# A 1-core transformer kernel: the first group of token attention in two halves, and weight loads issued behind the next rows' load

## The chip, the core and the metric

The kernel runs on one core of a Trainium2 chip. A core has a matmul engine (TensorE, PE in the profile), a vector engine (DVE), a scalar engine (ACT), GpSimd (POOL) and a sync engine (SP), which here issues all DMAs. Each engine works through its own instructions in order, and semaphores tie them together. The metric is the device time of one execution in microseconds (us).

## The reference

Three layers one after the other: attention over time steps inside each of 64 batches (the part that the change touches), a windowed attention over features, and a gated network with ternary weights.

```python
def _L0_tok_ref(qkv):                      # qkv is x: 64 x 96 x 512
    ch = qkv.shape[1] // 3                 # 32
    q, k, v = jnp.split(qkv, 3, axis=1)
    scale = 1.0 / np.sqrt(np.sqrt(ch)).astype(np.float32)
    weight = jnp.einsum('bct,bcs->bts', q * scale, k * scale)
    weight = jax.nn.softmax(weight.astype(jnp.float32), axis=-1).astype(weight.dtype)
    return jnp.einsum('bts,bcs->bct', weight, v)
...
h = _L0_tok_ref(x)
h = h + _L0_attn_ref(_layernorm(h, axis=-1), Wq, Wk, Wv, Wo, qn_w, kn_w)
h = h + _L0_ffn_ref(_layernorm(h, axis=-1), w1, w2, w3)
```

The second layer needs a scale for each attention weight matrix (from the largest absolute value), the third the mean absolute value of each of its matrices. The kernel measures both on the chip while the first layer runs.

## The kernel before

**Groups.** Token attention takes the 64 batches in 16 groups of 4 (`NG`, `GB`). A group has 16 (`STEPS`) row blocks and 16 column blocks of scores, each 128 x 512.

**Splitting and stacking.** The scores are made from fp32 numbers split in a high and a low part. `load_qk(g)` (L268) brings the raw q and k of a group (512 KB). ACT writes the high part (`raise_`, L418), POOL the low part (`lower`, L370), and `stack(g)` (L276 to L282) is six SBUF-to-SBUF copies of 256 KB that set high and low parts on interleaved partitions of `q_parts` and `k_parts`, 96 partitions in all. The raw rows of all groups but group 1 go through one buffer, `qk_split`, so `load_qk(g)` waits until `stack(g-1)` has landed.

**Rows, maxima, columns.** `rows(g, k)` (L625) makes one row block of scores; DVE reduces it to 128 row maxima (`maximum`, L473). After the 16 row blocks PE turns the maxima over (`transpose_maxima`, L631), DVE negates and splits them (`max_hi`, L480, and `max_lo`, L482), and SP stores them as partitions 96 and 97 of `q_parts` (`store_max`, L296, two DMAs of 8 KB). `cols(g, u)` (L640) makes the transposed scores with the maxima already subtracted; its first one in a group waits for both stores. ACT takes the exponentials (`exps`, L434), and `weigh(g, i)` (L650) multiplies four of them with v at the steps of `OUT_AT`. `total` (L659, L662) sums for the denominators.

**The order on PE.** The code is a hand-written pipeline. In group g, step u runs from 2 to 17. A step makes one row block of a later group (rows of group g+1 up to its last, then from step 11 on rows of group g+2), one column block (from step 16 on those of group g+1), and what `OUT_AT` adds. The transpose of the maxima of group g+1 stands in step 12. `score_ring` numbers the uses of the three PSUM banks of row scores in this order.

**The order on SP.** One queue, in program order. Round g of its loop: `stack(g+2)`, the v rows, the weight chunks that are measured in group g+1 (2 attention chunks of 512 KB where g+1 is even, 3 where it is odd, and 1 feed-forward chunk of 704 KB, up to group 7), `load_qk(g+3)`, the store of a finished group (`store_h`, 256 KB), and `store_max(g+1)`. The chunks of group 0 (2 and 1) are issued ahead of the loop. Their DMAs are L301 and L306.

**The order on ACT.** The exponentials step by step; after step 13 `raise_(g+3)`; the chunks' measurements (`bound_attn`, L438, and `sum_ffn`, L443) at the steps 3, 8, 12 and 5.

## Time and profile before

| | us |
|---|---|
| median of 3 runs | 1065.02 |
| lowest and highest of them | 1060.88, 1065.99 |
| the profiled execution's own time | 1062.14 |
| its span in the profile | 1060.3 |

| engine | busy us | share of the span |
|---|---|---|
| PE, matmul | 972.8 | 92% |
| DVE | 728.4 | 69% |
| POOL | 489.7 | 46% |
| ACT | 449.9 | 42% |

Token attention lies in the first 340 us or so; the two later layers fill the rest. A timeline row gives the start, the duration, the engine and source line, the tiles written and read, and in brackets how long the engine had been idle before and what ended that.

### The profile page before, as it was taken

What the parts mean: (1) busy time and instruction counts of PE and PEld (TensorE: products, weight loads), DVE (VectorE), ACT (ScalarE), POOL (GpSimd) and SP (SyncE); (2) the same over time, 40 slices, a digit from 0 to 9 for tenths busy, and PEclk for the clock granted to TensorE, in tenths of its full rate; (3) what the DMA queues carried; (4) which work ended last, traced back from release to release, by engine and by line L of the source; (5) the groups of instructions that cost most, each with busy time, mean ns of one, the idle gap of its engine ahead of it and who ended that gap; (6) DMA issues with size and microseconds to landing.
All of it is one profiled execution on the core that took longest, in us unless ns stands there. A gap on an engine that the chain in (4) does not pass through costs nothing.

```text
span 1060.3 us, 20456 instructions
## 1 busy us (share of the span) xinstructions
PE 972.8 (92%) x7799; PEld 523.1 (49%) x7799; DVE 728.4 (69%) x1265; ACT 449.9 (42%) x761; POOL 489.7 (46%) x373
## 2 busy tenths in 40 slices
PE   4998989887887589999999999999999999999986
PEld 1433333332332236566466564664655646646555
DVE  5675767887888877676675776766756767567542
ACT  1676766676775444333242233332432333323221
POOL 2243434355757764544346345443463454434500
PEclk9998999999998889999999999999999999999998
DMA  8996976667533313223223132231231322312300
GB/s 219 269 298 198 294 241 187 198 182 207 155 134 112 89 27 65 64 59 74 50 59 73 46 69 62 57 79 45 54 79 49 69 59 58 81 45 46 72 20 21
DMA packets 157483, 113.14 MB, mean 107 GB/s; under 512 B 126336, under 2 KB 126976, under 8 KB 157440
## 3 DMA queue, kind: packets, MB, share of 16 engines
q1 hardware_dynamic: 157440, 112.59, 39.5%
q8 instruction: 24, 0.39, 0.2%
q14 instruction: 19, 0.16, 0.0%
HBM read 49.36 MB, written 8.39 MB: 54 GB/s over the span
## 4 chain that ended last, share of the span: by engine, by line
PE 60%; issue 3%; DVE 3%; POOL 2%; DMA 1%; SPq 1%; ACT 1%; POOLq 0%; DVEq 0%; ACTq 0%
PE ffn_sum L1428 7%; PE ffn_sum L1429 7%; PE proj L1491 5%; PE proj L1486 5%; PE proj L1487 5%; PE proj L1375 4%; PE proj L1377 4%; PE proj L1376 4%; PE transposed L1457 3%; PE transposed L1458 3%; PE ffn_sum L1377 3%; PE ffn_sum L1376 3%; PE ffn_sum L1375 3%; PE ffn_sum L1471 2%; PE transposed L1375 1%
## 5 line engine op out<-in xcount | busy, mean ns | idle before, releaser
L1009 POOL TENSOR_TENSOR roped<-rope_cos,rope_sin 128x512 f32<-128x512 f32 x80 | 107.7, 1347 | 246.9 <-DVE rope_sin L1209 246.9
L473 DVE TENSOR_REDUCE row_max<-score_rows 128x1 f32<-128x512 f32 x256 | 163.0, 677 | 47.7 <-PE score_rows L625 47.7
L434 ACT ACTIVATE exps<-score_cols 128x512 f32<-128x512 f32 x256 | 140.2, 600 | 92.3 <-PE score_cols L640 89.4
L1428 PE MATMUL ffn_sum<-x_hi,ffn_w 128*128 128x128 f16 x1408 | 162.4, 221 | 8.0 <-DMA x_lo<-x_lo_rows 8.0
L1429 PE MATMUL ffn_sum<-x_lo,ffn_w 128*128 128x128 f16 x1408 | 162.2, 221 | 0.0
L625 PE MATMUL score_rows<-k_parts,q_parts 96*128 96x512 f32 x256 | 121.7, 491 | 29.4 <-DMA k_parts<-qk_split 14.1
L1428 PEld LDWEIGHTS ffn_sum<-x_hi,ffn_w 128*128 128x128 f16 x1408 | 138.0, 98 | 11.8 <-DMA x_lo<-x_lo_rows 8.4
L1429 PEld LDWEIGHTS ffn_sum<-x_lo,ffn_w 128*128 128x128 f16 x1408 | 138.6, 98 | 1.8
L640 PE MATMUL score_cols<-q_parts,k_parts 98*128 98x512 f32 x256 | 107.9, 429 | 12.7 <-DMA q_parts<-max_lo 7.8
L379 POOL TENSOR_TENSOR exp_sums<-exps 128x512 f32<-128x512 f32 x64 | 84.0, 1343 | 65.4 <-PE score_rows L625 39.3
L625 PEld LDWEIGHTS score_rows<-k_parts,q_parts 96*128 96x128 f32 x256 | 52.1, 205 | 120.4 <-DVE row_max L473 68.7
L1486 PE MATMUL proj<-attn_slots,ctx_hi 128*128 128x512 f16 x256 | 98.2, 383 | 4.8 <-ACT ctx_hi L1126 3.2
L1487 PE MATMUL proj<-attn_slots,ctx_hi 128*128 128x512 f16 x256 | 98.2, 384 | 0.0
L1021 POOL TENSOR_TENSOR roped_lo_rows<-roped,roped_hi_rows 128x512 f16<-128x512 f32 x77 | 90.5, 1192 | 0.0
L1092 ACT ACTIVATE squares<-ffn_sum 128x512 f32<-128x512 f32 x32 | 19.1, 598 | 159.9 <-PE ffn_sum L1377 159.9
L1363 DVE SCALAR_TENSOR_TENSOR h<-proj,o_unscale,h_res 128x512 f32<-128x512 f32 x16 | 12.0, 751 | 99.3 <-PE proj L1491 99.3
L1240 DVE SCALAR_TENSOR_TENSOR x2n_tanh_hidden<-x2n_tanh_hidden,ffn_sum 128x512 f32<-128x512 f32 (+1 forms) x48 | 30.8, 641 | 68.1 <-PE ffn_sum L1429 68.1
L1375 PE MATMUL proj<-attn_slots,x_hi 128*128 128x512 f16 x192 | 73.9, 385 | 3.3 <-DMA x_lo<-x_lo_rows 3.3
L650 PE MATMUL tok_out<-exps,v_t 128*32 128x512 f32 x512 | 72.2, 637 | 4.5 <-ACT exps L434 4.4
L1377 PE MATMUL proj<-attn_slots,x_lo 128*128 128x512 f16 x192 | 73.9, 385 | 0.0
L1376 PE MATMUL proj<-attn_slots,x_hi 128*128 128x512 f16 x192 | 73.9, 385 | 0.0
L90 POOL TENSOR_TENSOR attn_slots<-attn_slots 128x1024 f16<-128x1024 f32 x20 | 47.6, 2378 | 54.5 <-ACT attn_slots L86 54.5
(154 smaller groups left out, 1897.1 us busy)
## 6 DMA issues: line engine op xcount, KB each, us to landing
q_parts<-qk_split SPq DMA_DIRECT2D x45, 256.0 KB, 4.2
k_parts<-qk_split SPq DMA_DIRECT2D x45, 256.0 KB, 4.7
attn_slots<-in_w_attn SPq DMA_DIRECT2D x20, 512.0 KB, 7.0
ffn_w<-in_w_ffn SPq DMA_DIRECT2D x13, 704.0 KB, 8.3
qk_split<-in_qk SPq DMA_DIRECT2D x15, 512.0 KB, 5.9
raw_ffn<-in_w_ffn SPq DMA_DIRECT2D x8, 704.0 KB, 6.9
v_t<-in_v_t SPq DMA_DIRECT2D x16, 256.0 KB, 5.6
h_rows<-tok_out_sum SPq DMA_DIRECT2D x16, 256.0 KB, 3.4
```

The costliest lines, as they stand in the source:

```text
L434: nc.scalar.activation(E[:, n % NE, :], ST[n % 3][:, :], ACT.Exp, scale=TOK_SCALE).then_inc(exp_done, 1)
L473: nc.vector.reduce_max(row_max[:, g % 2, k:k + 1], S[n % NS][:, :], AX.X).then_inc(s_free, 1)
L625: nc.tensor.matmul(bank[:, :], QP[g % NB][0:3 * CH, b, t * P:(t + 1) * P], KP[g % NB][0:3 * CH, b, :], start=True, stop=True).then_inc(s_f ...
L640: nc.tensor.matmul(ST[n % 3][:, :], KP[g % NB][0:3 * CH + 2, b, i * P:(i + 1) * P], QP[g % NB][0:3 * CH + 2, b, :], start=True, stop=True) ...
L1009: nc.gpsimd.tensor_tensor(rope[:, c, :], ra[c % 2][:, :], rb[c % 2][:, :], ALU.add).then_inc(added, 1)
L1375: nc.tensor.matmul(dst, ah, bh, start=(i == 0), stop=False)
L1376: nc.tensor.matmul(dst, ah, bl, start=False, stop=False)
L1377: t = nc.tensor.matmul(dst, al, bh, start=False, stop=(i == len(pairs) - 1))
L1428: nc.tensor.matmul(dst, w, x2h[:, k, :], start=(k == 0), stop=False)
L1429: ins = nc.tensor.matmul(dst, w, x2l[:, k, :], start=False, stop=(k == KD - 1))
L1486: nc.tensor.matmul(PROJ[1][:, :], ch[:, k, :], W.hi(at, D), start=(k == 0), stop=False)
L1487: nc.tensor.matmul(PROJ[1][:, :], ch[:, k, :], W.lo(at, D), start=False, stop=False)
```

## The change

Four things change.

1. **The first group comes in halves.** The host lays out group 0 so that batches 0 and 1 are on the first 64 partitions. ACT raises q and k of group 0 apart, POOL lowers q and DVE lowers k. `stack_first` makes two times six copies of 128 KB, first for batches 0 and 1, then for 2 and 3. The row maxima of group 0 are turned over, split and stored in two halves of 8 row blocks each (`transpose_half`, `take_half`, `store_half_max`). The column blocks of group 0 are taken in the order of `FIRST_COLS`, whose first six need only the first half. PE makes 1 row block of group 1 instead of 7 before the first column block, and two in each of steps 2 to 6 (`rows_beside`).
2. **The queue of SP.** `stack(1)` is issued directly behind the copies of group 0. `load_qk(2)` moves behind the first half's maxima and the v rows of group 0, and `raise_(2)` behind the first two exponentials. In each round of the loop `load_qk(g+3)` stands in front of the weight chunks. The chunks of group 0 are no longer issued ahead of the loop but in round 0, together with those of group 1.
3. **The measurements.** ACT measures attention chunks at steps 4, 7 and 10 and the feed-forward chunk at step 15 (in group 0: 10 and 14, and 16).
4. **Waits.** Semaphore counts are moved by the one more raise and the one more pair of stores.

```diff
+HALF = STEPS // 2
+HALF_TAKE = HALF + 1
+FIRST_COLS = [(0, 0), (0, 1), (1, 0), (1, 1), (2, 0), (2, 1), (0, 2), (0, 3), (1, 2), (1, 3), (2, 2), (2, 3),
+              (3, 0), (3, 1), (3, 2), (3, 3)]
+SECOND_HALF = 6
+
+
+def col_of(g, u):
+
+    return FIRST_COLS[u] if g == 0 else divmod(u, GB)
+
+
+def exps_needed(g, pairs):
+
+    return STEPS * g + 1 + max(u for u in range(STEPS) if col_of(g, u) in pairs)
+
+
+def rows_beside(g, u):
+
+    if g == 0 and u < LOOK:
+        return [(1, 2 * u - 2), (1, 2 * u - 1)]
+    if u < MAX_AT:
+        return [(g + 1, u - 2 + LOOK)] if g + 1 < NG else []
+    return [(g + 2, u - MAX_AT)] if g + 2 < NG else []
+
...
 def score_ring():
 
-    entries = [("row", 0, k) for k in range(STEPS)]
-    for k in range(LOOK):
-        entries += [("row", 1, k)] + ([("max", 0)] if k == TAKE else [])
+    entries = []
+    for k in range(STEPS):
+        entries += [("row", 0, k)] + ([("half_max", 0)] if k == HALF_TAKE else [])
+    entries += [("row", 1, 0), ("row", 1, 1), ("max", 0)]
     for g in range(NG):
         for u in range(2, STEPS + 2):
-            if u < MAX_AT and g + 1 < NG:
-                entries.append(("row", g + 1, u - 2 + LOOK))
-            if u >= MAX_AT and g + 2 < NG:
-                entries.append(("row", g + 2, u - MAX_AT))
+            entries += [("row", *at) for at in rows_beside(g, u)]
             if u == MAX_AT + TAKE and g + 1 < NG:
                 entries.append(("max", g + 1))
...
-        A_MEASURE_AT, F_MEASURE_AT, CONVERT_AT = (3, 8, 12), (5,), (3, 12, 16, 8)
+        A_MEASURE_AT, F_MEASURE_AT, CONVERT_AT = (4, 7, 10), (15,), (3, 12, 16, 8)
+        FIRST_A_MEASURE_AT, FIRST_F_MEASURE_AT = (10, 14), (16,)
...
-        OUT_AT = {8: 0, 10: 1, 13: 2, 17: 3}
+        OUT_AT, FIRST_OUT_AT = {8: 0, 10: 1, 13: 2, 17: 3}, {9: 0, 11: 1, 13: 2, 17: 3}
...
                 if g == 2:
+                    sp.wait_ge(half_stacked, COPIES)
                     sp.wait_ge(stacked[0], copies(0))
...
+            def stack_first(half):
+                done, bs = (half_stacked, stacked[0])[half], slice(2 * half, 2 * half + 2)
+                of = slice(half * 2 * CH, half * 2 * CH + 2 * CH)
+                high, low = split_high(0).bitcast(FP32), split_low(0).bitcast(FP32)
+                sp.wait_ge(hi_done, 1)
+                sp.dma_start(QP[0][0:3 * CH:3, bs, :].bitcast(FP32), high[of, 0, :]).then_inc(done, DMA)
+                sp.dma_start(QP[0][1:3 * CH:3, bs, :].bitcast(FP32), high[of, 0, :]).then_inc(done, DMA)
+                sp.wait_ge(hi_done, 2)
+                sp.dma_start(KP[0][0:3 * CH:3, bs, :].bitcast(FP32), high[of, 1, :]).then_inc(done, DMA)
+                sp.dma_start(KP[0][2:3 * CH:3, bs, :].bitcast(FP32), high[of, 1, :]).then_inc(done, DMA)
+                sp.wait_ge(lo_done, 1)
+                sp.dma_start(QP[0][2:3 * CH:3, bs, :].bitcast(FP32), low[of, 0, :]).then_inc(done, DMA)
+                sp.wait_ge(k_lo_done, 1)
+                sp.dma_start(KP[0][1:3 * CH:3, bs, :].bitcast(FP32), low[of, 1, :]).then_inc(done, DMA)
+
             def load_v(g):
                 if g >= NV:
                     sp.wait_ge(out_done, NT * (g - NV + 1))
                 sp.dma_start(VT[g % NV][:, :, :].rearrange("p i n -> p (i n)"), vt[g, :, :]).then_inc(v_in[g % NV], DMA)
 
+            def store_half_max(half):
+                bs = slice(2 * half, 2 * half + 2)
+                for part, of in enumerate((max_hi, max_lo)):
+                    if part == 0:
+                        sp.wait_ge(max_split, half + 1)
+                    else:
+                        sp.wait_ge(s_free, ring["max" if half else "half_max", 0] + 1)
+                    row = QP[0][3 * CH + part:3 * CH + part + 1, bs, :].bitcast(FP32)
+                    sp.dma_start(row, of[0:HALF, :].bitcast(FP32)).then_inc(max_in, DMA)
+
...
             sp.dma_start(ident[:, :], ident_in).then_inc(ident_in_sem, DMA)
-            stack(0)
+            stack_first(0)
+            stack_first(1)
+            stack(1)
+            store_half_max(0)
+            load_v(0)
             load_qk(2)
-            stack(1)
-            load_v(0)
+            store_half_max(1)
             load_v(1)
-            for c in A_MEASURED[0]:
-                load_attn(c)
-            for c in F_MEASURED[0]:
-                measure_ffn(c)
-            store_max(0)
             for g in range(NG):
                 if g + 2 < NG:
                     stack(g + 2)
                 if 0 < g and g + 1 < NG:
                     load_v(g + 1)
+                if g + 3 < NG:
+                    load_qk(g + 3)
+                for c in A_MEASURED[0] if g == 0 else ():
+                    load_attn(c)
+                for c in F_MEASURED[0] if g == 0 else ():
+                    measure_ffn(c)
                 for c in A_MEASURED[g + 1] if g + 1 < NG else ():
                     load_attn(c)
                 for c in F_MEASURED[g + 1] if g + 1 < NG else ():
@@ -350,8 +406,6 @@
                     sp.wait_ge(h_out, DMA)
                     rows1.load(sp, 0, h1[0:P, :])
                     rows1.load_constants(sp, tables_in, norm_in, mask_in)
-                if g + 3 < NG:
-                    load_qk(g + 3)
                 if g > 0:
                     store_h(g - 1)
                 if g + 1 < NG:
...
         @block.scalar
         def _(act):
+            def raise_first(m):
+                act.wait_ge(qk_in[0], DMA)
+                nc.scalar.copy(split_high(0)[:, m, :], split_raw(0)[:, m, :]).then_inc(hi_done, 1)
+
             def raise_(g):
                 act.wait_ge(qk_in[g % 2], DMA * (g // 2 + 1))
                 if g == 2:
+                    act.wait_ge(half_stacked, COPIES)
                     act.wait_ge(stacked[0], copies(0))
...
                         act.wait_ge(s_full, ring["den", was] + 1)
-                if n == NE - 4:
+                i, b = col_of(g, u)
+                if g == 0 and (i, b) == (2, 0):
                     act.wait_ge(stacked[1], copies(1))
-                nc.scalar.activation(E[:, n % NE, :], ST[n % 3][:, :], ACT.Exp, scale=TOK_SCALE).then_inc(exp_done, 1)
+                nc.scalar.activation(E[:, (STEPS * g + GB * i + b) % NE, :], ST[n % 3][:, :], ACT.Exp, scale=TOK_SCALE).then_inc(exp_done, 1)
...
             def bound_attn(c):
                 act.wait_ge(a_in[c % NA], DMA * (c // NA + 1))
+                if c > 0:
+                    act.wait_ge(a_stat, c)
...
 
-            for g in range(3):
-                raise_(g)
+            raise_first(0)
+            raise_first(1)
+            raise_(1)
             exps(0, 0)
             exps(0, 1)
+            raise_(2)
             for g in range(NG):
                 for u in range(2, STEPS + 2):
                     if u < STEPS:
@@ -455,8 +525,8 @@
                         exps(g + 1, u - STEPS)
                     if u == SPLIT_AT and g + 3 < NG:
                         raise_(g + 3)
-                    for at, chunks, what in ((A_MEASURE_AT, A_MEASURED[g], bound_attn),
-                                             (F_MEASURE_AT, F_MEASURED[g], sum_ffn),
+                    for at, chunks, what in ((A_MEASURE_AT if g else FIRST_A_MEASURE_AT, A_MEASURED[g], bound_attn),
+                                             (F_MEASURE_AT if g else FIRST_F_MEASURE_AT, F_MEASURED[g], sum_ffn),
...
-            nc.vector.memset(ones[:, :], 1.0).then_inc(const_set, 1)
             for n in range(NB):
+                if n == 1:
+                    dve.wait_ge(hi_done, 2)
+                    nc.vector.tensor_tensor(split_low(0)[:, 1, :], split_raw(0)[:, 1, :], split_high(0)[:, 1, :].bitcast(FP32),
+                                            ALU.subtract).then_inc(k_lo_done, 1)
+                    nc.vector.memset(ones[:, :], 1.0).then_inc(const_set, 1)
...
-                    if k == TAKE and r >= 1:
+                    if (r, k) == (0, HALF_TAKE):
+                        take_half(0)
+                    if (r, k) == (1, TAKE):
+                        take_half(1)
+                    if k == TAKE and r >= 2:
...
-                if k == 0:
+                if (g, k) == (0, 0):
+                    pe.wait_ge(half_stacked, COPIES)
+                elif k == 0 or (g, k) == (0, HALF):
                     pe.wait_ge(stacked[g % 2], copies(g))
                 bank = enter_ring(ring["row", g, k])
...
 
+            def transpose_half(half):
+                last = half * HALF + HALF
+                pe.wait_ge(s_free, ring["row", 0, last - 1] + 1)
+                bank = enter_ring(ring["max" if half else "half_max", 0])
+                nc.tensor.transpose(bank[0:HALF, 0:P], row_max[:, 0, last - HALF:last], ident[:, :]).then_inc(s_full, 1)
...
-                    pe.wait_ge(max_in, 2 * DMA * (g + 1))
+                i, b = col_of(g, u)
+                if (g, u) == (0, 0):
+                    pe.wait_ge(const_set, 1 + NB)
+                    pe.wait_ge(max_in, 2 * DMA)
+                elif u == 0 or (g, u) == (0, SECOND_HALF):
+                    pe.wait_ge(max_in, 2 * DMA * (g + 2))
                 if n >= 3:
...
+                out_at = FIRST_OUT_AT if g == 0 else OUT_AT
+                if u in out_at:
+                    weigh(g, out_at[u])
...
 
-            pe.wait_ge(ident_in_sem, DMA)
-            pe.wait_ge(const_set, 1 + NB)
             for k in range(STEPS):
                 rows(0, k)
-            for k in range(LOOK):
-                rows(1, k)
-                if k == TAKE:
-                    transpose_maxima(0)
+                if k == HALF_TAKE:
+                    pe.wait_ge(ident_in_sem, DMA)
+                    transpose_half(0)
+            rows(1, 0)
             cols(0, 0)
+            rows(1, 1)
+            transpose_half(1)
...
```

**SP's queue from the last stacking copy of group 2 to the maxima of group 1, before.** L282 is that copy, L301 and L306 are weight chunks, L268 the raw rows of group 3, L296 the maxima:

```order
L282 DMA k_parts<-qk_split 32x4x512
L301 DMA attn_slots<-in_w_attn 128x1024 x3
L306 DMA ffn_w<-in_w_ffn 128x1408
L268 DMA qk_split<-in_qk 128x1024 [waits t_stacked0]
L296 DMA q_parts<-max_hi 1x16x128 [waits t_max_split]
L296 DMA q_parts<-max_lo 1x16x128 [waits t_s_free]
```

The same piece now (L309 the last copy, L295 the raw rows, L353 and L358 the chunks, L348 the maxima):

```order
L309 DMA k_parts<-qk_split 32x4x512
L295 DMA qk_split<-in_qk 128x1024 [waits t_stacked0]
L353 DMA attn_slots<-in_w_attn 128x1024 x2
L358 DMA ffn_w<-in_w_ffn 128x1408
L353 DMA attn_slots<-in_w_attn 128x1024 x3
L358 DMA ffn_w<-in_w_ffn 128x1408
L348 DMA q_parts<-max_hi 1x16x128 [waits t_max_split]
L348 DMA q_parts<-max_lo 1x16x128 [waits t_s_free]
```

The raw rows have moved ahead of the chunks, and three chunks (two attention, one feed-forward) have come in that stood ahead of this piece before.

**SP's queue ahead of that piece, now:** from the last copy of group 1 (L309) over the maxima of the two halves (L339), the v rows (L329) and the raw rows of group 2 (L295) to the first copy of group 2 (L303):

```order
L309 DMA k_parts<-exps 32x4x512
L339 DMA q_parts<-max_hi 1x8x128 [waits t_max_split]
L339 DMA q_parts<-max_lo 1x8x128 [waits t_s_free]
L329 DMA v_t<-in_v_t 128x512
L295 DMA qk_split<-in_qk 128x1024 [waits t_stacked0,t_half_stacked]
L339 DMA q_parts<-max_hi 1x8x128 [waits t_max_split]
L339 DMA q_parts<-max_lo 1x8x128 [waits t_s_free]
L329 DMA v_t<-in_v_t 128x512
L303 DMA q_parts<-qk_split 32x4x512 [waits t_hi_done]
```

Before, the v rows, two attention chunks and a feed-forward chunk stood between the copies of group 1 and one pair of maxima, and the raw rows of group 2 were issued ahead of the copies of group 1.

**ACT in group 0, before** (L434 exponentials, L438 attention chunk, L443 feed-forward chunk):

```order
L434 ACTIVATE exps<-score_cols 128x512 [waits t_st_done] x4
L438 ACTIVATE attn_slots,w_bound<-attn_slots 128x1024 [waits w_a_in0]
L434 ACTIVATE exps<-score_cols 128x512 [waits t_st_done] x2
L443 ACTIVATE ffn_w,w_fsum<-ffn_w 128x1408 [waits w_fm_in0]
L434 ACTIVATE exps<-score_cols 128x512 [waits t_st_done] x2
```

and now (L483 is the raise, L500 the exponentials, L506 the attention chunk):

```order
L500 ACTIVATE exps<-score_cols 128x512 [waits t_st_done] x2
L483 CAST qk_split<-qk_split 128x1024 [waits t_stacked0,t_half_stacked,t_qk_in0]
L500 ACTIVATE exps<-score_cols 128x512 [waits t_st_done] x2
L500 ACTIVATE exps<-score_cols 128x512 [waits t_stacked1,t_st_done]
L500 ACTIVATE exps<-score_cols 128x512 [waits t_st_done] x6
L506 ACTIVATE attn_slots,w_bound<-attn_slots 128x1024 [waits w_a_in0]
L500 ACTIVATE exps<-score_cols 128x512 [waits t_st_done]
```

The raise of group 2 has come in behind the second exponential, and the first chunk is measured behind the eleventh instead of the fourth.

## Rows read from the trace of the kernel before

**Rows 1.** Stretch, length, busy PE, PEld, DVE, ACT, POOL; granted clock, DMA share, GB/s.
```profile
400.00:1060.00 660.00, 645.21 (x6121) 388.06 (x6119) 426.26 (x783) 204.98 (x360) 289.09 (x245) 0.99 0.26 58
```

**Rows 2.** Timeline, all engines, from the start to the first column block.
```profile
5.03 0.71 SPq L276 DMA_DIRECT2D q_parts<-qk_split  x1
...
8.38 0.61 SPq L282 DMA_DIRECT2D k_parts<-qk_split  x1
...
14.12 9.52 PE L625 MATMUL score_rows<-k_parts,q_parts 96*128 96x512 f32 x16 [14.12 <-DMA k_parts<-qk_split]
...
20.98 0.43 SPq L306 DMA_DIRECT2D ffn_w<-in_w_ffn  x1
...
25.06 1.22 PE L625 MATMUL score_rows<-k_parts,q_parts 96*128 96x512 f32 x2 [1.43 <-DMA k_parts<-exps]
...
27.10 0.27 DVE L480 TENSOR_SCALAR max_hi<-score_rows 16x128 fp32r<-16x128 f32 x1
...
31.62 1.22 PE L640 MATMUL score_cols<-q_parts,k_parts 98*128 98x512 f32 x2 [1.89 <-DMA q_parts<-max_lo]
```

**Rows 3.** Timeline, PE, group 0: columns 6, third weighing, first columns of group 1.
```profile
36.48 0.63 PE L640 MATMUL score_cols<-q_parts,k_parts 98*128 98x512 f32 x1
...
43.16 1.06 PE L650 MATMUL tok_out<-exps,v_t 128*32 128x512 f32 x8
...
45.79 0.50 PE L640 MATMUL score_cols<-q_parts,k_parts 98*128 98x512 f32 x1 [0.20 <-DMA q_parts<-max_lo]
```

**Rows 4.** Timeline, SP: issues of round 0, then of round 2.
```profile
28.67 0.61 SPq L276 DMA_DIRECT2D q_parts<-qk_split  x1
...
37.86 0.33 SPq L268 DMA_DIRECT2D qk_split<-in_qk  x1
...
63.01 0.61 SPq L276 DMA_DIRECT2D q_parts<-qk_split  x1
...
71.92 0.33 SPq L268 DMA_DIRECT2D qk_split<-in_qk  x1
...
78.24 0.59 SPq L296 DMA_DIRECT2D q_parts<-max_lo  x1
```

**Rows 5.** DMA issues of 18 to 31.6 us: count, KB each, median us to landing.
```profile
ffn_w<-in_w_ffn SPq DMA_DIRECT2D x1, 704.0 KB, 10.1
q_parts<-max_hi SPq DMA_DIRECT2D x1, 8.0 KB, 3.2
q_parts<-max_lo SPq DMA_DIRECT2D x1, 8.0 KB, 3.5
```

**Rows 6.** The same for single issues: at 78.24, 134.84 and 164.40 us.
```profile
q_parts<-max_lo SPq DMA_DIRECT2D x1, 8.0 KB, 3.6
...
q_parts<-max_lo SPq DMA_DIRECT2D x1, 8.0 KB, 1.9
...
qk_split<-in_qk SPq DMA_DIRECT2D x1, 512.0 KB, 3.2
```

**Rows 7.** Busy time by stretch, columns as in rows 1.
```profile
36.90:43.60 6.70, 6.70 (x36) 2.94 (x38) 4.89 (x10) 6.60 (x13) 4.89 (x4) 1.00 1.02 402
79.40:81.80 2.40, 0.57 (x3) 0.13 (x1) 1.54 (x3) 0.97 (x2) 0.00 (x0) 0.96 0.07 22
81.80:88.00 6.20, 6.16 (x19) 2.40 (x23) 2.08 (x3) 3.33 (x8) 2.37 (x1) 0.50 0.82 191
```

**Rows 8.** Timeline, PE: the first columns of groups 2, 3, 4 and 7.
```profile
62.93 0.50 PE L640 MATMUL score_cols<-q_parts,k_parts 98*128 98x512 f32 x1 [0.18 <-DMA q_parts<-max_lo]
...
81.84 0.80 PE L640 MATMUL score_cols<-q_parts,k_parts 98*128 98x512 f32 x1 [1.87 <-DMA q_parts<-max_lo]
...
102.62 0.50 PE L640 MATMUL score_cols<-q_parts,k_parts 98*128 98x512 f32 x1 [0.95 <-DMA q_parts<-max_lo]
...
155.48 0.50 PE L640 MATMUL score_cols<-q_parts,k_parts 98*128 98x512 f32 x1 [1.84 <-DMA q_parts<-max_lo]
```

**Rows 9.** Timeline, ACT: the raise of group 5.
```profile
80.83 1.04 ACT L418 CAST qk_split<-qk_split 128x1024 fp32r<-128x1024 f32 x1 [2.60 <-DMA qk_split<-in_qk]
```

51 lines of the change are left out of this document (31 added, 20 removed).

## The prediction

> **What bounds the kernel now.** I read the busy times first. From 400 us to the end PE is busy 645 of 660 us [rows 1], and nothing there is tied to a clock time, so whatever moves the end of token attention moves the end of the kernel by as much. So the question is when each group's first column block starts. I call that moment C0 for group 0, C1 for group 1, and so on.
>
> Next the timeline of the start. The first stacking copy is issued at 5.03, the sixth at 8.38, and the row blocks start at 14.12: 9.1 us after the first issue. They run at one per 0.6 us. Group 1's copies hold the next rows until 25.06, the maxima are split at 27.10 and C0 is 31.62 [rows 2]. C1 is 45.79 [rows 3]. C1 to C2 takes 17.14 us, and PE waited only 0.2 us for the maxima there [rows 3, 8]: the undisturbed pace of a group. C3 and C7 come late, each after an idle PE of 1.9 us behind the maxima's store [rows 8].
>
> Then the DMA engines. The copies are slow, the loads fast: from 36.90 to 43.60 the loads of round 0 move 402 GB/s at a DMA share of 1.02 [rows 7]. They are full, and the maxima's store goes into the same queue. An 8 KB store lands in 1.9 us when the queue is empty, in 3.5 to 3.6 us when weight chunks are ahead of it [rows 5, 6].
>
> **The start (half stacking).** A half is six copies of 128 KB. SP issues one per 0.67 us (3.35 us for five steps [rows 2]), so the first half is issued from about 4.6 to 8.6 us and lands near 10.7. The rows of batches 0 and 1 hide the second half: eight blocks of 0.6 us against 4 us of issue. Twelve issues end at 12.5, stack(1) is issued by 16.4. All three move 3.15 MB; one stack of 1.57 MB took 9.1 us of which I take 7.3 for its bytes, so stack(1) lands near 21. The first half's maxima are ready at 17.8 but their store is queued behind stack(1), so it lands at about 21.8, and **C0 is 22.0, 9.6 us earlier**. PE is then six row blocks behind the old order. They cost DVE time in steps 2 to 6: five steps with two blocks, ten of 0.65 us, from 24.4. Column block 6 comes at 29.7 against 36.48 [rows 3]. The second half's maxima (split at 24.2, landed near 26.7) are in time. So 6.8 us are left of the gain there. Bounds: stack(1) cannot land before its last issue plus 3.2 us, 19.5 (C0 at 20.3); if 128 KB copies have a fixed cost of their own, C0 is 24.
>
> **Round 0 (the weights moved).** This is where I expect the gain to go. raise_(2) now stands behind the second exponential, which is done at 24.9, so stack(2) is issued from 26.2 (C0 + 4.2). A stack's landing frees load_qk 8.9 to 9.2 us after its first issue [rows 4]: 35.2 us. Only behind load_qk(3) do the chunks come, and they are five attention and two feed-forward chunks instead of three and one. First bytes come about 0.9 us after the issue (an estimate: 1.9 us for 8 KB, part of it before the first byte). From 36.1: 0.52 + 5 x 0.52 + 2 x 0.72 = 4.6 MB at 402 GB/s is 11.4 us, so the engines are full until 47.5. store_max(1) stands behind all of them on SP and in the queue. It would be issued at 39, in time for a C1 of 39.0 (29.7 + the 9.3 us from 36.48 to 45.79 [rows 3]). It lands 2 us behind the end of the backlog: in round 2 the loads ended at 79.4 and PE went on at 81.84 (2.4 us) [rows 7, 8], and at the start the store of max_lo landed 3.5 us after its issue [rows 5]. So **C1 is 49.5, 3.7 us later than before** instead of 6.8 earlier. Bounds: t(stack 2) from C0 at 20.3 gives 47.8, C0 at 24 gives 51.5; a price of zero for the backlog is the first rival below.
>
> ACT waits too: attention chunk 0 is measured at step 10, at 33.5 us, but lands at 35.2 + 3.2 + 1.3 = 39.7. With 1.3 us for the measurement the eleventh exponential ends at 41.6, and the third weighing waits for it, some 3 us. That lies inside the wait for C1 and costs nothing as long as the store lands later than 44.2.
>
> The order of landing in the queue rests on two stores, so I weighed it against a page. The feed-forward chunk issued at 20.98 landed 10.1 us later, at 31.1; max_hi, issued after the split at 27.4, landed 3.2 us later at 30.6, so ahead of the chunk, max_lo at 31.5, behind it [rows 2, 5]. The Trainium skill (DMA: Bandwidth & Descriptors, "Queues, rings and completion order") says that each DMA engine takes its descriptors in ring order, but that completion is not first in, first out over a queue. The trace agrees, with half a microsecond. By that rule C1 would be up to 1 us earlier, 48.5.
>
> **After C1.** PE stands idle for about 5.5 us (from 44 to 49.5). After the 1.87 us before C3, the granted clock was 0.50 for the next 6.2 us [rows 7], the lower of its two levels, 1.2 GHz; C3 to C4 took 20.78 us, 3.64 over the pace, of which 0.77 is the longer wait at C4 [rows 8]. So the clock cost 2.9. I put 2.9 behind C1. Bounds: 0 and 2.9.
>
> **Rounds 1 to 6.** Taking load_qk out of the tail removes the wait of ACT at 80.83 [rows 9]. But in before that wait ran beside the wait for the maxima, which ended later, at 81.84 [rows 8]. It is not worth anything alone. What sets C3 is the end of the backlog: stack issued 63.01, loads ended 79.4, 16.4 later [rows 4, 7]. Now the chunks wait for the stack to land. Between the v rows' last bytes and load_qk's first the engines stand still, 1.0 us (bounds 0.6 and 1.9, the whole latency of a small store). The same bytes then end 17.4 us after the stack's issue and the store lands 2.2 later, at 19.6. The stack is issued 0.8 us before C2, since no measurement stands at step 12 any more, so the store lands 18.8 us after it against a pace of 17.1: **a wait of 1.7 us in each round with three attention chunks** (2, 4, 6). With two chunks 1.3 us less is to be moved, and nothing waits. Before, waits of 1.87 and 1.84 us lowered the clock, one of 0.95 didn't [rows 8]; I count two thirds of 2.9 us for each of the two that fall between C2 and C7. That is 3 x 1.7 + 2 x 1.9 = 9.0 us over the pace between C2 and C7, where before had 92.55 - 5 x 17.14 = 6.85 [rows 8]. So **2.1 us more**. The measurements' new steps, the self-wait of bound_attn and the halved raises lie beside PE work and cost nothing; ACT has 42% of the span.
>
> **Sum.** 3.7 + 2.9 + 2.1 = 8.7 us. Against the execution's own 1062.1 that is 1070.8 us; the median of the runs is 2.9 us above that execution. I say 1071; this case's own range is 1066 to 1077.
>
> **The rivals.**
> 1. The store passes the weights (it waits for little more than its own 1.9 us). Then ACT's late measurement sets C1 at 41.6 + 2.6 = 44.2, 1.6 earlier than before, no clock is lost and rounds 2 to 6 run at the pace: -1.6 - 6.85 = -8.5, **1053.6**. It decides if the store of group 1's maxima lands within 5 us of its issue. For it: a max_hi landed ahead of an older chunk. Against it: both stores with chunks ahead took 3.5 us, not 1.9. Chance 0.14 (with other ways of a gain).
> 2. C1 is late as forecast, but the later rounds keep the pace, because ring order hurts less with load_qk gone from the tail: 3.7 + 2.9 - 6.85 = -0.3, **1062**. Chance 0.25.
> 3. C1 late and the waits of 1.7 us come, but the clock stays up after them: 6.6 + 5.1 - 6.85 = +4.9, **1067**. Chance 0.15.
> 4. The waits also come with two chunks (0.7 us each) and every one lowers the clock, or C0 is 24: +14, **1076**. Chance 0.10.
> 5. The forecast, 1071: 0.36.
>
> **How the numbers follow.** About 0.5% (5.3 us) is what a measurement of this kernel can tell from no change. Faster by more: rival 1 and the low tail of rival 2, 0.17. Within: the rest of rival 2, most of rival 3 and the low edge of the forecast, 0.35. Slower: 0.48. The range leaves out rival 1 and the far end of rival 4: 1056 to 1078.
>
> **What would show it.** C0 near 22; the first half's rows from 10.7; the raw rows of group 3 issued near 35; PE idle before C1 "<-DMA q_parts<-max_lo" for over 4 us, with the DMA share at 1.0 until 47 and the granted clock at 0.50 after it; C1 near 49.5; waits of 1 to 2 us before C3, C5 and C7. A C1 before 46 breaks the forecast, and so does a store of group 1's maxima that lands within 5 us.

## The result and the profile after

| | before | after |
|---|---|---|
| median of the runs, us | 1064.99 | 1083.7 |
| lowest and highest, us | 1060.88, 1065.99 | 1079.23, 1088.35 |
| runs | 4 | 4 |

The ratio is 1.0199, with a 95% interval of 1.014 to 1.0257: the changed kernel is slower by 2%. The prediction was 1071 with a range up to 1078. The sign was right and the size too small by more than half. The profiled execution took 1088.35 us, with a span of 1086.5. Some executions of a kernel are over 1.5% longer than its fastest; the ratios here and below leave these out, and two of the four of f1_before_order, its traced one (1088.22 us) among them, are such.

The later layers are as they were. The same length of time near the end, now shifted by 20 us, against [rows 1] (columns as there):

```profile
420.00:1080.00 660.00, 648.74 (x6138) 390.03 (x6137) 428.92 (x790) 206.17 (x362) 290.72 (x248) 0.99 0.26 59
```

So the loss is in token attention. PE at the start, against [rows 2, 3]: the first row blocks, the first column block, and column block 6, counted from 0 as the 36.48 of [rows 3] is.

```profile
10.88 5.96 PE L715 MATMUL score_rows<-k_parts,q_parts 96*128 96x512 f32 x10 [10.88 <-DMA k_parts<-qk_split]
...
23.17 0.70 PE L739 MATMUL score_cols<-q_parts,k_parts 98*128 98x512 f32 x1
...
30.40 0.39 PE L739 MATMUL score_cols<-q_parts,k_parts 98*128 98x512 f32 x1
```

Rows start at 10.88, C0 is 23.17 instead of 31.62, and column block 6 comes 6.1 us earlier than before. The halves do what they are meant to do. Then SP in round 0 and round 2, against [rows 4]:

```profile
27.09 0.62 SPq L303 DMA_DIRECT2D q_parts<-qk_split  x1
...
36.11 0.33 SPq L295 DMA_DIRECT2D qk_split<-in_qk  x1
36.49 0.91 SPq L353 DMA_DIRECT2D attn_slots<-in_w_attn  x2
...
70.35 0.60 SPq L303 DMA_DIRECT2D q_parts<-qk_split  x1
...
79.26 0.33 SPq L295 DMA_DIRECT2D qk_split<-in_qk  x1
79.63 1.38 SPq L353 DMA_DIRECT2D attn_slots<-in_w_attn  x3
...
81.55 0.45 SPq L373 DMA_DIRECT2D h_rows<-tok_out_sum  x1
...
85.92 0.66 SPq L348 DMA_DIRECT2D q_parts<-max_lo  x1
87.43 0.62 SPq L303 DMA_DIRECT2D q_parts<-qk_split  x1
```

The raw rows are issued 9.0 and 8.9 us after the first stacking copy, and the chunks directly behind them. PE and ACT next, against [rows 3, 8]: ACT at the first chunk, and PE at the third weighing and the first column blocks of groups 1, 3, 5 and 7.

```profile
41.13 1.06 ACT L506 ACTIVATE attn_slots<-attn_slots 128x1024 f32<-128x1024 f32 x1 [6.22 <-DMA attn_slots<-in_w_attn]
...
42.81 1.69 PE L749 MATMUL tok_out<-exps,v_t 128*32 128x512 f32 x8 [2.16 <-ACT exps L500]
...
51.24 0.80 PE L739 MATMUL score_cols<-q_parts,k_parts 98*128 98x512 f32 x1 [4.44 <-DMA q_parts<-max_lo]
...
94.11 0.80 PE L739 MATMUL score_cols<-q_parts,k_parts 98*128 98x512 f32 x1 [6.49 <-DMA q_parts<-max_lo]
...
133.03 0.79 PE L739 MATMUL score_cols<-q_parts,k_parts 98*128 98x512 f32 x1 [3.33 <-DMA q_parts<-max_lo]
...
173.67 0.80 PE L739 MATMUL score_cols<-q_parts,k_parts 98*128 98x512 f32 x1 [4.20 <-DMA q_parts<-max_lo]
```

C1 is 5.5 us late. The waits before C3, C5 and C7 are 6.49, 3.33 and 4.20 us, where before had 1.87 and 1.84 at C3 and C7 and 0.95 at C4. Busy time of the six groups from C2 to C8 (length; then PE, PEld, DVE, ACT, POOL; granted clock, DMA share, GB/s):

```profile
70.75:94.11 23.36, 16.14 (x89) 6.70 (x89) 13.32 (x24) 14.50 (x26) 8.88 (x6) 0.93 0.95 264
94.11:112.81 18.70, 17.74 (x90) 7.14 (x90) 11.76 (x21) 12.59 (x23) 5.96 (x5) 0.90 0.52 172
112.81:133.03 20.22, 16.14 (x89) 6.69 (x89) 13.31 (x24) 14.46 (x26) 8.86 (x6) 0.97 0.93 267
133.03:152.58 19.55, 18.59 (x90) 7.58 (x90) 11.84 (x21) 12.70 (x23) 5.96 (x5) 0.86 0.72 203
152.58:173.67 21.09, 16.14 (x90) 6.69 (x90) 13.31 (x24) 14.47 (x26) 8.88 (x6) 0.98 0.93 270
173.67:193.38 19.71, 18.76 (x90) 7.58 (x90) 11.85 (x21) 12.70 (x23) 5.96 (x5) 0.85 0.35 97
```

A group that begins behind a long wait shows a mean clock of 0.85 to 0.90 and takes 18.7 to 19.7 us instead of 17.1; a group with three chunks ends in the wait and takes 20.2 to 23.4. In the groups with three chunks the DMA engines are busy 93 to 95% of the time. C2 to C8 is 122.6 us against 111.3 before. C8 is 193.38 against 174.26, 19.1 us late, and the medians differ by 18.7: about all of the loss is there by C8. The two traced executions are 26.2 us apart, since from C8 to the last weighing the changed kernel took 168.2 us and before 160.3. But that stretch takes 154 to 169 us in the seventeen traces used here, with no order that follows the edits. From here on C8 and the stretch from C2 to C8 are what I compare.

Round 2 in pieces (columns as above):

```profile
79.00:80.00 1.00, 0.52 (x2) 0.30 (x2) 1.00 (x3) 1.00 (x3) 0.76 (x2) 1.00 0.24 86
80.00:81.00 1.00, 1.00 (x9) 0.16 (x8) 1.00 (x3) 1.00 (x2) 1.00 (x2) 1.00 0.75 176
81.00:86.00 5.00, 5.00 (x31) 2.06 (x27) 4.18 (x9) 3.87 (x9) 2.25 (x2) 1.00 1.05 369
86.00:88.00 2.00, 1.62 (x9) 0.87 (x5) 1.45 (x4) 1.87 (x4) 1.08 (x1) 1.00 0.94 351
88.00:90.00 2.00, 0.00 (x0) 0.00 (x0) 0.62 (x2) 1.41 (x3) 1.27 (x1) 1.00 1.00 329
90.00:94.00 4.00, 0.00 (x0) 0.00 (x0) 0.00 (x0) 0.00 (x0) 0.00 (x0) 0.61 1.06 228
```

From 79 to 80 the DMA engines nearly stand still. Then they load at 369 and 351 GB/s. PE stops at 88, and by 90 the rate has fallen to 228 GB/s: that is the six copies of the next stack, issued from 87.43 on, in front of which the maxima's store still has not landed. The granted clock goes to its lower level while PE stands.

The last two transfers in front of the store are the feed-forward chunk, issued at 81.07, and the h rows, issued at 81.55 (columns as in [rows 6]):

```profile
ffn_w<-in_w_ffn SPq DMA_DIRECT2D x1, 704.0 KB, 11.9
h_rows<-tok_out_sum SPq DMA_DIRECT2D x1, 256.0 KB, 12.1
```

They land at 93.0 and 93.7, and PE goes on at 94.11. In all rounds that I read this way (round 2 of before, after, e1, e4, f1, g1 and g4, rounds 4 and 6 of after and e4) PE went on 0.3 to 0.6 us after the h rows had landed. So the store lands with the last of the transfers in front of it, which can be some 2 us after most engines are through.

### The profile page after: what moved, and what is told of

The parts are those of the page before. It is cut to its first block, busy times and chain, and to the rows that moved or that the text cites. A ratio compares the mean times of both kernels' runs of the same rounds, so it can differ in the third digit from the quotient of the medians.

```text
span 1086.5 us, 20494 instructions
## 1 busy us (share of the span) xinstructions
PE 986.5 (91%) x7800; PEld 527.1 (49%) x7800; DVE 728.3 (67%) x1268; ACT 452.2 (42%) x762; POOL 487.5 (45%) x373
## 4 chain that ended last, share of the span: by engine, by line
PE 58%; issue 3%; DVE 3%; POOL 2%; DMA 1%; SPq 1%; ACT 1%; POOLq 0%; DVEq 0%; ACTq 0%
PE ffn_sum L1526 7%; PE ffn_sum L1527 7%; PE proj L1589 5%; PE proj L1584 5%; PE proj L1585 4%; PE proj L1473 4%; PE proj L1474 4%; PE proj L1475 4%; PE transposed L1555 3%; PE transposed L1556 3%; PE ffn_sum L1475 3%; PE ffn_sum L1473 3%; PE ffn_sum L1474 3%; PE ffn_sum L1569 2%; PE transposed L1473 1%
## 5 line engine op out<-in xcount | busy, mean ns | idle before, releaser
L500 ACT ACTIVATE exps<-score_cols 128x512 f32<-128x512 f32 x256 | 141.9, 598 | 126.3 <-PE score_cols L739 123.8
L715 PE MATMUL score_rows<-k_parts,q_parts 96*128 96x512 f32 x256 | 124.1, 498 | 27.4 <-DMA k_parts<-qk_split 12.7
L739 PE MATMUL score_cols<-q_parts,k_parts 98*128 98x512 f32 x256 | 111.7, 443 | 28.0 <-DMA q_parts<-max_lo 20.0
L438 POOL TENSOR_TENSOR exp_sums<-exps 128x512 f32<-128x512 f32 x64 | 82.1, 1309 | 89.3 <-PE score_rows L715 75.7
L715 PEld LDWEIGHTS score_rows<-k_parts,q_parts 96*128 96x128 f32 x256 | 53.5, 209 | 123.1 <-DVE row_max L543 64.6
L1190 ACT ACTIVATE squares<-ffn_sum 128x512 f32<-128x512 f32 x32 | 19.1, 598 | 159.6 <-PE ffn_sum L1475 159.6
L749 PE MATMUL tok_out<-exps,v_t 128*32 128x512 f32 x512 | 76.0, 669 | 4.6 <-ACT exps L500 4.5
L739 PEld LDWEIGHTS score_cols<-q_parts,k_parts 98*128 98x128 f32 x256 | 52.6, 207 | 50.3 <-DMA q_parts<-max_lo 28.5
```

The source lines that it names most:

```text
L500: nc.scalar.activation(E[:, (STEPS * g + GB * i + b) % NE, :], ST[n % 3][:, :], ACT.Exp, scale=TOK_SCALE).then_inc(exp_done, 1)
L715: nc.tensor.matmul(bank[:, :], QP[g % NB][0:3 * CH, b, t * P:(t + 1) * P], KP[g % NB][0:3 * CH, b, :], start=True, stop=True).then_inc(s_f ...
L739: nc.tensor.matmul(ST[n % 3][:, :], KP[g % NB][0:3 * CH + 2, b, i * P:(i + 1) * P], QP[g % NB][0:3 * CH + 2, b, :], start=True, stop=True) ...
```

## Experiments

The tables give the start of the first column blocks C1 and C8, the wait before C1 and those before C3, C5 and C7, the length from C2 to C8 (all from the profiled execution), and the time and ratio to the kernel before. Runs of one batch were on one chip; the kernel before had 1057.88 us (first four), 1061.3 (next four), 1060.45 (next four) and 1060.34 (last three). The column "us" is the median of all executions of a kernel: 2 for g1 and h1, 4 for before, after, e2, e4, f1 and f3, 10 or 12 for the others.

| kernel | C1 | wait C1 | waits C3, C5, C7 | C2 to C8 | C8 | us | ratio (interval) |
|---|---|---|---|---|---|---|---|
| before | 45.79 | 0.20 | 1.87, 0.17, 1.84 | 111.3 | 174.3 | 1064.99 | 1 |
| after | 51.24 | 4.44 | 6.49, 3.33, 4.20 | 122.6 | 193.4 | 1083.7 | 1.0199 (1.014 to 1.0257) |
| e1_order_back | 47.31 | 4.63 | 1.54, 0.21, 1.66 | 107.9 | 177.0 | 1061.64 | 1.0027 (0.9989 to 1.0066) |
| e2_chunks_early | 47.54 | 1.79 | 5.51, 3.13, 4.66 | 121.6 | 187.8 | 1075.52 | 1.0163 (1.0097 to 1.023) |
| e3_both | 43.91 | 0.32 | 1.47, 0.18, 1.75 | 108.9 | 173.3 | 1061.8 | 1.003 (0.9993 to 1.0067) |
| e4_copies_wait | 50.77 | 3.68 | 4.16, 3.53, 4.85 | 123.1 | 194.0 | 1081.63 | 1.0213 (1.0133 to 1.0293) |
| f1_before_order | 49.04 | 3.37 | 4.78, 3.74, 4.25 | 122.5 | 191.0 | 1083.0 | 1.0131 (1.0069 to 1.0193) |
| f2_before_actstore | 45.35 | 0.25 | 1.38, 0.95, 1.80 | 106.4 | 168.9 | 1057.13 | 0.9952 (0.9921 to 0.9984) |
| f3_after_actstore | 47.53 | 1.04 | 0.16, 0, 0; see below | 115.8 | 186.2 | 1070.91 | 1.0102 (1.0062 to 1.0142) |
| f4_both_actstore | 44.70 | 0 | 1.23, 0.40, 1.68 | 108.2 | 170.7 | 1057.97 | 0.9984 (0.9951 to 1.0018) |
| g1_half_chunks | 48.77 | 4.94 | 1.62, 0.97, 0.16 | (see below) | | 1072.65 | 1.0106 (1.001 to 1.0203) |
| g2_h_behind | 45.36 | 0.17 | 1.18, 0.51, 1.32 | 112.0 | 174.6 | 1060.88 | 0.9989 (0.9944 to 1.0035) |
| g3_h_behind_act | 45.54 | 0.23 | 1.49, 1.00, 1.56 | 114.5 | 177.1 | 1061.21 | 0.9997 (0.9958 to 1.0037) |
| g4_one_ahead | 48.59 | 7.31 | 2.73, 2.09, 2.70 | 115.1 | 182.3 | 1070.44 | 1.0105 (1.0063 to 1.0146) |
| h1_act_copies_wait | 48.25 | 0.94 | 2.09, 3.41, 3.87 | 120.7 | 191.1 | 1079.0 | 1.0179 (1.0111 to 1.0246) |
| h2_steps_actstore | 45.41 | 0.23 | 1.68, 0.15, 1.72 | 110.9 | 173.9 | 1056.54 | 0.9976 (0.995 to 1.0001) |
| h3_steps_only | 45.95 | 0.17 | 1.69, 0.18, 1.66 | 109.4 | 172.5 | 1057.21 | 0.9977 (0.9946 to 1.0009) |

### Which part of the change: undoing the order, undoing the place of group 0's chunks, both

Two theories after the result: A, the stacking copies of the next group get ahead of the maxima's store; B, the raw rows' place leaves the engines idle for 1 us.

e1_order_back:

```diff
-                if g + 3 < NG:
-                    load_qk(g + 3)
                 for c in A_MEASURED[0] if g == 0 else ():
...
+                if g + 3 < NG:
+                    load_qk(g + 3)
                 if g > 0:
                     store_h(g - 1)
```

> The changed kernel with load_qk(g+3) moved back behind the weight chunks in every round of the loop; all else as changed. Theory A (the next stacking copies are now issued right behind the maxima's store and get ahead of it, because the raise no longer waits for rows at the tail of the queue): the waits before the first columns of groups 3, 5 and 7 (6.5, 3.3 and 4.2 us in the changed kernel) fall to at most 2 us, since the raise is gated by the tail again; the first columns of group 1 stay near 50 us, and the time falls by 8 to 13 us, to about 1072. Theory B (only the idle gap of about 1 us before load_qk in the DMA engines matters): each of the three waits falls by 1 us, the time by 3 to 5 us, to about 1079.

The rounds go back to what they were before, or better: C2 to C8 takes 107.9 us, and the ratio goes from 1.0199 to 1.0027. That is far more than theory B's 3 to 5 us, and more than theory A's 8 to 13 too: C1, which was to stay near 50, is 3.9 us earlier. C1 to C2 takes 21.8 us here, since `load_qk(3)` stands behind seven chunks in round 0.

e2_chunks_early issues group 0's three chunks ahead of the loop, behind `load_qk(2)`:

```diff
             load_qk(2)
+            for c in A_MEASURED[0]:
+                load_attn(c)
+            for c in F_MEASURED[0]:
+                measure_ffn(c)
             store_half_max(1)
```

> The changed kernel with the three weight chunks of group 0 issued ahead of the loop again, behind load_qk(2); all else as changed. Both theories: the backlog in front of group 1's maxima is 1.77 MB smaller, 4.4 us at 402 GB/s, so the first columns of group 1 come at about 47 instead of 51.2 us, and PE's wait there shrinks from 4.4 to below 1 us; the time falls by 4 to 7 us, to about 1078. If the rounds' delay does not depend on when the first ends, the waits of groups 3, 5 and 7 stay at 3 to 6 us. If the chunks of group 0 are not the cause of the late group 1, nothing changes.

C1 comes 3.7 us earlier, behind a wait of 1.79 us where under 1 was expected, and that is all: the waits of the later rounds stand. The two parts are separate, and the second is the small one.

e3_both has both edits, so that of the change the halves, the place of the first stacking copies and the new measurement steps are left.

> Both of the two edits before: load_qk behind the weight chunks and the chunks of group 0 ahead of the loop; what is left of the change is the half-wise start, the stacking order at the start, and the measuring steps. Theory A: the sum of the two gains, 12 to 20 us, so at or below the kernel before: 1060 to 1070, with the first columns of group 1 near 43 us (before 45.8). Theory B: 1072 to 1076.

C1 is 1.9 us earlier than before, all that is left of a C0 that is 8 us earlier, and C2 gives it back: C1 to C2 takes 20.45 us. PE in group 0 and ACT at the raise of group 3:

```profile
36.73 0.73 PE L715 MATMUL score_rows<-k_parts,q_parts 96*128 96x512 f32 x1 [2.47 <-DMA k_parts<-qk_split]
...
43.53 1.05 ACT L483 CAST qk_split<-qk_split 128x1024 fp32r<-128x1024 f32 x1 [1.64 <-DMA qk_split<-in_qk]
```

The copies of group 2 hold PE for 2.47 us at 36.73, and the raise of group 3 waits for its rows at 43.53. The early start meets a supply that has not become earlier.

e4_copies_wait tests theory A: the copies of the next group wait until the maxima have landed.

```diff
+                if 0 < g and g + 2 < NG:
+                    sp.wait_ge(max_in, 2 * DMA * (g + 2))
                 if g + 2 < NG:
                     stack(g + 2)
```

> The changed kernel with one more wait on the issuing queue: stack(g+2) is issued only when both stores of group g's maxima have landed (from round 1 on); the order of the loads stays as changed. Theory A: the copies can no longer get ahead of the store, so the waits before groups 3, 5 and 7 fall from 6.5, 3.3 and 4.2 us to 2 to 2.5 us, the time by 4 to 8 us. Theory B, or a store that is late only because of the chunks in front of it: the waits keep their length, the stacking comes later, and the time stays or grows by up to 5 us.

The wait before C3 falls by 2.3 us, those before C5 and C7 do not, and the time stays. Theory A is not the main cause. With the copies gone from the tail, round 2 can be read cleanly: first copy issued at 70.85, most engines through with the loads at 89.5, C3 at 91.92.

```profile
79.00:81.00 2.00, 1.40 (x10) 0.46 (x10) 2.00 (x4) 2.00 (x5) 1.75 (x3) 1.00 0.51 132
81.00:86.00 5.00, 5.00 (x31) 2.06 (x27) 4.17 (x9) 3.87 (x9) 2.37 (x2) 1.00 0.97 360
86.00:89.00 3.00, 1.76 (x9) 0.87 (x5) 2.21 (x4) 2.87 (x5) 1.95 (x1) 1.00 0.96 330
89.00:90.00 1.00, 0.00 (x0) 0.00 (x0) 0.00 (x0) 0.54 (x2) 0.40 (x1) 1.00 0.53 198
90.00:92.00 2.00, 0.08 (x1) 0.08 (x1) 0.00 (x0) 0.00 (x0) 0.00 (x0) 0.75 0.10 37
```

The h rows, issued at 83.12, land at 91.5 here:

```profile
h_rows<-tok_out_sum SPq DMA_DIRECT2D x1, 256.0 KB, 8.4
```

### The order alone, on the kernel before

f1_before_order:

```diff
+                if g + 3 < NG:
+                    load_qk(g + 3)
                 for c in A_MEASURED[g + 1] if g + 1 < NG else ():
                     load_attn(c)
...
-                if g + 3 < NG:
-                    load_qk(g + 3)
                 if g > 0:
                     store_h(g - 1)
```

> The kernel before with one edit: in each round of SP's loop the raw rows' load (load_qk(g+3)) stands in front of the weight chunks. Theory C (the order alone is the cause: the chunks wait until the stack has landed, so their bytes end right at the maxima's store): C2 to C8 takes 120 to 124 us instead of 111.3, C1 comes up to 2 us later since group 0's three chunks still go ahead of the loop, waits of 3 to 6 us stand before C3, C5 and C7, and the time is 1070 to 1077 where before has 1058 to 1065, so a ratio of 1.009 to 1.014. Theory D (the order costs only together with the new measurement steps and the halves): C2 to C8 takes 113 us or less and the ratio is under 1.004.

C2 to C8 takes 122.5 us, as in the changed kernel. One line of order in the queue makes the whole loss of the rounds; e1 says the same from the other side. f1's traced execution took 1088.22 us where two others took 1070.52 and 1077.78, but 897 us of it lie behind C8, against 888 in before, so much of the extra length is not in the rounds. In time the order alone costs 1.3%, less than the 2.0% of the whole change, with intervals that overlap. Its C1 is 3.3 us later than before, where up to 2 were expected. Round 2 of the undone order (e1, first copy issued at 68.72) and of the order alone (f1, 68.42), first e1, then f1:

```profile
77.00:79.00 2.00, 1.25 (x11) 0.46 (x10) 2.00 (x5) 2.00 (x6) 1.76 (x2) 1.00 1.02 376
79.00:85.00 6.00, 6.00 (x37) 2.49 (x30) 4.69 (x9) 4.12 (x8) 2.59 (x3) 1.00 1.02 408
85.00:87.00 2.00, 0.96 (x5) 0.44 (x3) 1.88 (x3) 0.52 (x1) 0.00 (x0) 1.00 0.12 40
```

```profile
77.00:79.00 2.00, 1.76 (x11) 0.55 (x11) 2.00 (x5) 2.00 (x6) 2.00 (x3) 1.00 0.51 130
79.00:88.00 9.00, 6.46 (x32) 2.83 (x32) 6.01 (x11) 5.76 (x10) 4.09 (x3) 1.00 1.00 355
88.00:90.00 2.00, 0.00 (x0) 0.00 (x0) 0.00 (x0) 0.00 (x0) 0.00 (x0) 0.65 1.06 219
```

In e1 the chunks are already queued when the copies are through, so the engines pass to them without a break, move 376 to 408 GB/s and most are through at 85.1. In f1 they move 130 GB/s for two microseconds, then 355, and are not through when the next copies (issued at 85.25) come in at 88; then it is 219 GB/s.

### How much a byte in front of the store costs

g1_half_chunks:

```diff
-                sp.dma_start(W.raw(c), w_attn[:, c * A_CHUNK:(c + 1) * A_CHUNK])
+                sp.dma_start(W.raw(c)[:, 0:A_CHUNK // 2], w_attn[:, c * A_CHUNK:c * A_CHUNK + A_CHUNK // 2])
...
+                if g == 7:
+                    for c in range(A_CHUNKS):
+                        load_rest(c)
```

> The changed kernel, but each attention chunk's load in the rounds brings half of its columns (256 KB), and only that half is measured; the other halves are all loaded in round 7, so only groups 0 to 7 are to be compared. Measuring the second halves is left out. Theory G (the waits are the length of the backlog that stands between the stack's landing and the maxima): a round with three chunks has 0.79 MB less, 2.1 to 2.3 us at 340 to 385 GB/s, so the waits before C3, C5, C7 fall from 6.5, 3.3, 4.2 to about 4, 1.2, 2.0, the one before C1 (five chunks, 1.3 MB less) from 4.4 to 1, and C2 to C8 is 110 to 116 us instead of 122.6. Theory H (the waits come from the order of issue and landing as such, or from the next stack's copies): they change by less than 0.7 us each, C2 to C8 stays over 119 us.

The three waits fall by 4.9, 2.4 and 4.0 us, 3.8 on the mean, more than the 2.1 to 2.3 us of the bytes; a new wait of 1.24 us before C6 takes some of it back, so that the waits from C3 to C7 fall by 3.4 us a round. C2 to C7 takes 91.6 us (102.9 in the changed kernel, 92.6 before). C8 cannot be used, since the other halves are loaded there. The wait before C1, which was to fall to 1 us, rose from 4.44 to 4.94: C1 itself is 2.5 us earlier, but PE reached it at 43.8 instead of 46.8, since ACT began on the first chunk 1.6 us sooner and measured only half of it, and the copies of group 3 were issued from 43.63 on, again ahead of the landing. A likely reason for the surplus is in the windows: most engines are through with round 2 at 83.9, before the copies issued at 84.08 move a byte.

```profile
78.00:84.00 6.00, 6.00 (x32) 2.68 (x31) 4.62 (x10) 4.17 (x7) 2.04 (x3) 1.00 0.96 339
84.00:85.00 1.00, 0.28 (x2) 0.00 (x0) 1.00 (x3) 1.00 (x3) 1.00 (x1) 1.00 0.11 35
```

g2_h_behind and g3_h_behind_act take 256 KB from the front of the store in the kernel before, g3 with the maxima on ACT's queue. g2:

```diff
-                if g > 0:
-                    store_h(g - 1)
                 if g + 1 < NG:
                     store_max(g + 1)
+                if g > 0:
+                    store_h(g - 1)
```

> The kernel before, with the finished group's h rows (256 KB) stored behind the maxima instead of in front of them. Theory G: 0.26 MB less backlog, 0.65 us at 402 GB/s, so the waits before C3 and C7 are 1.2 us instead of 1.87 and 1.84 and C4's goes to 0.3; where the clock then stays up, another 2.9 us each, so 2 to 8 us less, ratio 0.992 to 0.998. Theory H or no effect: ratio 0.999 to 1.002. If the h store then delays the next stack's copies, the rows of the group behind wait and the ratio is over 1.002.

> The kernel before with the maxima's stores on ACT's queue and the h rows stored just ahead of the next stack, so behind the maxima. Theory G: the waits of 1.38, 0.95 and 1.80 us before C3, C5 and C7 with ACT's queue alone fall by 0.65 us each, ratio 0.988 to 0.994. If the DMA engines' whole load of a round sets the time, not what stands ahead of the store, the ratio stays at 0.995 as with ACT's queue alone.

In g2 the waits fall by 0.7 and 0.5 us, as the bytes say, but the group behind C3 still takes 19.4 us: after a wait of 1.18 us the clock fell all the same, here two microseconds later.

```profile
80.97:83.00 2.03, 1.53 (x7) 0.64 (x11) 0.69 (x1) 2.03 (x5) 1.28 (x1) 1.00 0.01 4
83.00:87.00 4.00, 4.00 (x20) 1.48 (x16) 1.38 (x2) 1.86 (x5) 1.09 (x1) 0.57 1.06 247
```

In g3 nothing is won: the waits are those of ACT's queue alone (f2, below) within 0.3 us, and the 0.5% of f2 is gone too. In both, a ratio of 0.998 or less was expected and did not come.

g4_one_ahead puts one chunk of each round in front of the raw rows:

```diff
+                ahead = A_MEASURED[0] if g == 0 else A_MEASURED[g + 1][:1] if g + 1 < NG else ()
+                for c in ahead:
+                    load_attn(c)
                 if g + 3 < NG:
                     load_qk(g + 3)
```

> The changed kernel with one attention chunk of each round issued in front of the raw rows (in round 0 the two of group 0), so that the engines have bytes to move while SP waits for the stack to land. Theory J (the standing still of the DMA engines between the stack and the raw rows is what is lost, near 2 us a round): filled by 0.5 MB, so the rounds with three chunks take 19 us or less instead of 21.6, C2 to C8 is 112 to 115 us, and the time is 1066 to 1072. Theory K (every byte that is issued behind the landing counts alike): a chunk of four pieces is 1.3 us of it, C2 to C8 falls by 1.3 us in each three-chunk round and by the clock behind waits that fall under 1.9 us, so 115 to 119 us and 1073 to 1078.

C2 to C8 is 115.1 us and the time 1070.4: the far edge of J and the near edge of K. In round 2 there is no break, 351 GB/s from 75 to 78; most engines are through with them at 84.1, just ahead of the next copies:

```profile
75.00:78.00 3.00, 2.26 (x13) 0.93 (x13) 3.00 (x6) 3.00 (x8) 2.76 (x3) 1.00 0.98 351
78.00:84.00 6.00, 5.99 (x31) 2.46 (x30) 4.63 (x10) 4.72 (x9) 2.34 (x3) 1.00 0.99 356
84.00:85.00 1.00, 0.00 (x0) 0.00 (x0) 0.98 (x2) 1.00 (x2) 1.00 (x1) 1.00 0.22 78
```

None ahead 122.6 us, one chunk ahead 115.1, all ahead 107.9 (e1): the loss goes down step by step with what is queued behind the stack. The wait of 7.31 us before C1 is no contradiction: PE reached it at 41.28, and C1 is 2.7 us earlier than in the changed kernel.

### Is it the queue or the engines

f2, f3 and f4 take the maxima's stores off SP's queue (f2 on the kernel before, f3 on the changed one, f4 on e3). ACT issues them behind the exponential of step 13:

```diff
+                    if u == SPLIT_AT and g + 1 < NG:
+                        store_max_act(g + 1)
                     if u == SPLIT_AT and g + 3 < NG:
                         raise_(g + 3)
```

> The kernel before with one edit: the two stores of the maxima of groups 1 to 15 are issued by ACT, on its own DMA queue, behind the exponential of step 13, not by SP behind the chunks. Theory E (place in the queue: the store is late because older bytes of the same queue go first): it lands about 2 us after its issue whatever the loads do, the waits of 1.87, 0.95 and 1.84 us before C3, C4 and C7 go, and with them the clock's 2.9 us after two of them; C2 to C8 is 103 to 105 us instead of 111.3, and the time 6 to 8 us less, ratio 0.993. Theory F (the DMA engines are full, and it is their load, not the queue, that makes the store late): the waits stay within 0.5 us and the ratio is 0.999 to 1.002. ACT's two issues cost it a few tenths of a us each; if they push the exponentials, C0 to C1 grows and the ratio is over 1.003.

> The changed kernel with the same edit: the stores of the maxima of groups 1 to 15 on ACT's own queue. Theory E: the waits of 4.4, 6.5, 3.3 and 4.2 us before C1, C3, C5 and C7 fall to under 1 us, C2 to C8 is 103 to 106 us instead of 122.6, C1 is near 47 (ACT's late chunk still holds the third weighing), and the time is 1055 to 1062, ratio 0.997 to 1.003. Theory F: waits as in the changed kernel within 1 us, time 1078 to 1084.

> The changed kernel with the chunks of group 0 ahead of the loop, the raw rows' load behind the chunks in each round, and the stores of the maxima on ACT's queue. Theory E: C1 43.7 as without the ACT queue, C2 to C8 103 to 105 us instead of 108.9, no waits before C3 and C7, ratio 0.992 to 0.996. Theory F: as without the ACT queue, ratio 1.000 to 1.005.

In f2 the waits hardly fall; it is 0.5% faster, about the least that can be told here, and the only kernel whose interval lies below 1. Of the 4.9 us that C2 to C8 is shorter, 3.6 lie between C3 and C4 and 1.6 between C7 and C8: behind waits of 1.38 and 1.80 us the granted clock stayed at 1.00 here. h2, with the same stores, does not repeat it (110.9 us). f4 is no better. f3 comes down from a ratio of 1.0199 to 1.0102, but waits have moved to the groups with two chunks: 6.03 us before C2, 3.43 before C4, 3.13 before C6. The timeline of f3 has the store (ACT's queue) and the first column block of group 2 behind it:

```profile
62.70 0.88 ACTq L507 DMA_DIRECT2D q_parts<-max_lo  x1
...
70.49 0.79 PE L748 MATMUL score_cols<-q_parts,k_parts 98*128 98x512 f32 x1 [6.03 <-DMA q_parts<-max_lo]
```

and the DMA engines meanwhile:

```profile
64.00:66.00 2.00, 0.46 (x2) 0.02 (x1) 1.45 (x3) 2.00 (x4) 1.20 (x1) 1.00 0.93 344
66.00:70.00 4.00, 0.00 (x0) 0.00 (x0) 0.00 (x0) 1.07 (x2) 1.16 (x1) 0.55 1.05 256
```

A store on a queue of its own took 7.8 us from its issue to PE's start, beside copies issued from 64.80 on. The h rows of that round were issued at 59.38 on SP's queue:

```profile
h_rows<-tok_out_sum SPq DMA_DIRECT2D x1, 256.0 KB, 11.3
```

They landed at 70.7 and the chunk ahead of them at 70.1, so the store again landed with the last of the loads. h1_act_copies_wait holds those copies back, with the wait of e4 in f3:

> The changed kernel with the maxima's stores on ACT's queue, as before, and SP holds the next group's six stacking copies until those stores have landed. Theory L (on its own queue the store is held only by the copies that start while it is under way, which fill the engines at 230 to 250 GB/s): the store before C2 lands within 3 us of its issue, the wait of 6.0 us there falls under 2, and the ones of 3.4 and 3.1 us before C4 and C6 too. Theory M (it is held by the whole backlog whichever queue it is on): the wait before C2 stays over 3.5 us, and the later ones within 1 us of what they were.

The wait before C2 is 2.62 us, between what the two theories said. The store is issued at 66.08 and PE goes on at 70.46; most engines are through with the loads at about 68.3, and the h rows land at 70.0. So both count: even on its own queue the store lands with the last of the loads, and where the next copies start before that, all of them land later. Before C4 and C6 the waits do fall under 2 us (1.35, 0.74), as theory L said. The waits before C5 and C7 come back (3.41, 3.87), and with them most of the time: the larger part of what f3 had won was that SP issued the next copies without waiting for the maxima. Against e4, which holds the copies with the store on SP's queue, h1 is 2.4 us shorter from C2 to C8 and C1 is 2.5 us earlier; that is what the queue is worth there.

### The measurement steps

h3 has `A_MEASURE_AT = (4, 7, 10)`, `F_MEASURE_AT = (15,)` and the self-wait on the kernel before, h2 also the store of f2.

> The kernel before with the new measurement steps alone. They lie beside PE work: ratio 0.997 to 1.001, C2 to C8 108 to 112 us, waits before C3 and C7 as before within 0.4 us.

> The kernel before with the changed kernel's measurement steps (attention chunks at 4, 7 and 10, the feed-forward chunk at 15, and the self-wait) and the maxima's stores on ACT's queue. If the new steps spare what the trace of the undone order showed (C2 to C8 107.9 us where before has 111.3, C3 to C4 18.2 instead of 20.8): C2 to C8 105 to 107 us, ratio 0.991 to 0.996. If they are worth nothing: ratio 0.995 to 0.998, as ACT's queue alone, which had 0.995.

Both are the same as before within the interval. The new steps cost nothing and bring at most a few tenths of a per cent.

## Why the prediction was right in its direction and wrong in its size

**The start** was right. C0 was 23.17 for 22.0 (within the bound of 24), column block 6 was 30.40 for 29.7, so that 6.1 us of the gain were left there for 6.8, and the first half had landed at 10.88 for 10.7.

**Round 0** was right in its mechanism and 1.7 us short. The issues came at 27.09 and 36.11 for 26.2 and 35.2, and C1 at 51.24 for 49.5, inside the upper bound of 51.5. Not foreseen was that the copies of group 2 held PE for 1.87 us at 36.14, with a lowered clock behind it. ACT waited for chunk 0 until 41.13, and the third weighing came at 42.81, for 41.6. e2 shows what the three moved chunks cost at C1: 3.7 us. The rival that the store passes the weights falls by its own test: max_lo was issued at 41.41 and PE went on at 51.24, 9.8 us later, where it allowed 5.

**After C1** the clock was as said: C1 to C2 took 19.51 us, 2.4 over the pace for 2.9 forecast.

**Rounds 1 to 6 are the step that failed**, in the term "a wait of 1.7 us in each round with three attention chunks". The waits were 6.49, 3.33 and 4.20 us, 4.7 on the mean. From C2 to C7, 102.9 us, 17.2 over the pace: 13.2 of the waits' excess and 4.0 of the clock, where I had 5.1 and 3.8. The clock's term was right to 0.2 us, the waits' was less than half. By the chain that I used:

- I had the loads end 17.4 us after the stack's first issue. In e4, where no copies disturb them, it was 18.7 (70.85 to 89.5). Two numbers were too good there. The break: the full rate begins at 81.0, 10.2 us after the first issue, with 132 GB/s in the two microseconds before. And the rate: I took 402 GB/s from round 0, and in round 2 it was 330 to 360 in e4, 355 in f1, 369 and 351 in the changed kernel. In the changed kernel's own round 0 it was 392 (38 to 49 us), so the figure was right for that round only.
- PE went on 2.4 us behind that, for 2.2: the h rows landed only at 91.5, and the store with them.
- The stack was issued 0.4 us ahead of C2, C4 and C6, for 0.8.
- What I left out: the late end of the loads runs into the next stack's copies, and together they move 228 GB/s. From the stack's issue to C the changed kernel took 23.8, 20.6 and 21.5 us, 22.0 on the mean, against 21.1, 20.4 and 21.7, also 21.1 on the mean, in e4. So the 0.9 us is a mean of 2.7 in round 2 and about nothing in rounds 4 and 6.

Together 1.3 + 0.2 + 0.4 + 0.9 = 2.8 us a round on top of 1.7, which is the wait measured over the pace (22.0 - 0.4 - 17.1 = 4.5). How much of the first term is the break and how much the rate no run tells apart. The rule cited in the prediction, that the engines take descriptors in ring order, led to the right order of events, but it made me look at the queue. The same section of the Trainium skill (DMA: Bandwidth & Descriptors, "Queues, rings and completion order") also says that an engine goes round between its queue rows packet by packet. That sentence alone let me expect the store of f3 to pass the loads; the page does not promise it. It did not pass them: it took 7.8 us in f3 and 4.4 us in h1, and landed with the last of the loads in both. No run shows why.

**Rival 2**, that the later rounds keep the pace because the raw rows have left the tail, had 0.25 and is wrong by f1: it is just that move that costs 11 us between C2 and C8. Rival 4, waits with two chunks too, is wrong in its mechanism (0.2 us before C2, C4 and C6), though its price came nearest. In all: +5.5 at C1, +2.4 to C2 and +11.3 to C8 are 19.1; I had 3.7, 2.9 and 2.1.

The sum also had a slip in its base: I added the 8.7 us to the traced execution's 1062.1 and not to the median, and then did not add the 2.9 us between the two. On the median of 1065.0 it gives 1073.7, still 10 us short.

The range failed with the term of the waits. I had given the break bounds and the rate none, and I had not asked what a backlog of 18 us meets when the next round's copies come after 17.

## What to carry to other kernels

Where a queue's tail holds a small transfer that someone waits for, ask when the last of the transfers under way will have landed, on whichever queue they are. A load that waits on a semaphore and stands in front of loads that wait for nothing makes all of them late; put those without a wait first, so that the engines have work while the issuer waits. And a backlog that is nearly as long as the period is to be priced by what it runs into, not by its bytes.

## What the runs showed of the hardware

- The SBUF-to-SBUF copies and the loads both keep the DMA engines busy nearly all of the time (shares of 0.94 to 1.06), but the copies move 217 to 228 GB/s (e4 from 75 to 79 us, after from 90 to 94) and the loads 330 to 408 (e4, e1). Where the copies came in before the loads had landed, the last two transfers of round 2 took 11.9 and 12.1 us to land (after); where they were held, 8.3 and 8.4 (e4).
- The rate of the loads differed with the same bytes: in round 2 it was 408 GB/s in e1, where they were queued before the copies ended, 355 in f1, where they were issued behind the copies, but also 356 in g4, where one chunk filled the break. In round 0 of the changed kernel it was 392, though all were issued into idle engines. So the time of issue alone does not explain it. Why is open.
- An 8 KB store on ACT's own queue was hardly faster through full engines than on SP's: 7.8 us before C2 in f3, 8.2 us before C3 in the changed kernel (issued at 85.92). With the copies held it took 4.4 us on ACT's queue (h1) and 5.9 on SP's (e4, issued at 86.06, round 2, which has a chunk more).
- The granted clock went to its lower level after the waits of over 3 us, and the group behind took 1.6 to 2.6 us over the pace in the changed kernel. After shorter waits the length alone did not decide: it fell after 1.87 us in before and after 1.18 us (and another 0.50 just behind it) in g2, but stayed at 1.00 after 1.38 and 1.80 us in f2, and after 1.04 us before C4 in e1, where the groups behind took 17.20, 17.18 and 17.08 us.
